# Sandwich block with attention-like scan and top-2 experts, one core: first statistics of batches 4 to 7 and the second tile table placed ahead of tile 0

## The reference

```python
# x: 8 batches x 512 tokens x 128
x = x + layernorm(attn(layernorm(x)))
x = x + layernorm(ffn(layernorm(x)))

def attn(x):                      # a scan over the tokens, not softmax attention
    inp = mix * x + (1 - mix) * shifted(x)          # shifted by one token
    h = relu(inp @ W_in.T + b_in)
    state_t = state_{t-1} * decay + h_t             # along the 512 tokens
    return states @ W_out.T + b_out

def ffn(x):                       # 8 experts, 128 -> 512 -> 128, top 2
    weights = softmax(top2(x @ gate))
    y_e = (silu(x @ w0[e]) * (x @ w1[e])) @ wo[e]
    return sum over the two chosen experts of weight * y_e
```

## Time and profile before

| | us |
|---|---|
| median of 3 executions | 274.52 (274.36 to 274.54) |
| profiled execution | 274.19 |
| its span, first to last instruction | 272.4 |
| TensorE busy | 243.0 (89%) |
| VectorE busy | 186.1 (68%) |
| ScalarE busy | 179.0 (66%) |
| GpSimd busy | 167.2 (61%) |

### The profile page before, as it was taken

One profiled execution on the slowest core, in us unless ns is written; L12 is line 12 of the kernel. 1 busy time (PEld: TensorE's weight loads), 2 busy tenths in 40 slices (PEclk: granted clock), 3 DMA queues, 4 the chain that ended last, 5 costly groups with the idle time before them and its releaser, 6 DMA issues.

```text
span 272.4 us, 8097 instructions
## 1 busy us (share of the span) xinstructions
PE 243.0 (89%) x2059; PEld 231.2 (85%) x2059; DVE 186.1 (68%) x815; ACT 179.0 (66%) x517; POOL 167.2 (61%) x190
## 2 busy tenths in 40 slices
PE   7948778899898999999999999999999999999800
PEld 2738655799898999999999999999999999999700
DVE  4886876877785785687578687844353434998774
ACT  2185869577576777785867587655656566568581
POOL 3317774773678878778878878776333324277740
PEclk9997799999999999999999999999999999999955
DMA  5999961413301321132123113433322108403048
GB/s 174 300 358 375 292 215 51 101 52 84 106 32 49 88 84 40 62 96 65 40 71 101 49 45 108 110 90 89 82 78 70 51 28 331 178 16 96 13 152 231
DMA packets 29675, 31.70 MB, mean 116 GB/s; under 512 B 4778, under 2 KB 22188, under 8 KB 29504
## 3 DMA queue, kind: packets, MB, share of 16 engines
q1 hardware_dynamic: 24448, 22.56, 27.7%
q0 software_dynamic: 4320, 8.50, 8.9%
q10 hardware_dynamic: 864, 0.13, 0.3%
HBM read 19.58 MB, written 12.05 MB: 116 GB/s over the span
## 4 chain that ended last, share of the span: by engine, by line
PE 73%; DVE 14%; issue 4%; POOL 4%; ACT 2%; DVEq 1%; POOLq 0%
PE bank L1764 40%; PE bank L1801 21%; PE bank L1715 3%; PE bank L1759 2%; DVE sb_early L1001 2%; PE bank L1810 2%; PE bank L1665 1%; POOL expert_rows L524 1%; ACT sb_square L653 1%; DVE sb_w_now L1387 1%; DVEq L1381 1%; DVE sb_rest_stats L983 1%; PE bank L1683 1%; POOL pair_rows L537 1%; DVE sb_x L1016 1%
## 5 line engine op out<-in xcount | busy, mean ns | idle before, releaser
L1764 PE MATMUL bank<-sb_xeT,sb_w_now 128*128 128x128 f32 x1136 | 139.5, 275 | 2.9 <-DVE sb_gated L1368 2.4
L1764 PEld LDWEIGHTS bank<-sb_xeT,sb_w_now 128*128 128x128 f32 x1136 | 133.0, 192 | 3.8 <-issue 3.8
L537 POOL DMA_INDIRECT pair_rows<-sb_y_rows,sb_y_pair x71 | 73.4, 1033 | 53.3 <-ACT sb_y_rows L777 32.3
L1368 DVE TENSOR_TENSOR sb_gated<-bank,sb_silu 128x512 f32<-128x512 f32 x71 | 48.9, 689 | 58.0 <-PE bank L1764 46.8
L524 POOL DMA_INDIRECT expert_rows<-sb_row,sb_place x64 | 64.8, 1012 | 28.9 <-issue 18.1
L1801 PE MATMUL bank<-sb_w_raw,sb_gated 128*128 x568 | 75.7, 276 | 0.4 <-ACT sb_y_rows L777 0.3
L1801 PEld LDWEIGHTS bank<-sb_w_raw,sb_gated 128*128 128x128 f32 x568 | 69.1, 192 | 1.0 <-issue 0.9
L748 ACT ACTIVATE sb_silu<-bank 128x512 f32<-128x512 f32 x71 | 42.3, 595 | 17.2 <-PE bank L1764 16.9
L743 ACT ACTIVATE sb_xeT<-bank 128x128 f32<-128x128 f32 x71 | 19.4, 274 | 40.8 <-PE bank L1759 40.5
L766 ACT ACTIVATE sb_w_now<-sb_w_raw 128x512 f32 x71 | 44.3, 624 | 0.0
L1387 DVE COPY sb_w_now<-sb_w_raw 128x512 f32 x71 | 30.2, 425 | 1.6 <-issue 1.6
(11 more groups left out here) (203 smaller groups left out, 249.8 us busy)
## 6 DMA issues: line engine op xcount, KB each, us to landing
sb_taken_rows<-expert_rows SPq DMA_DIRECT2D x71, 65.5 KB, 1.9
sb_w_raw<-in_L_ffn_w SPq DMA_DIRECT2D x2, 2048.0 KB, 16.2
sb_pairs_early<-pair_rows SPq DMA_DIRECT2D x3, 1024.0 KB, 7.2
out_dram<-sb_x SPq DMA_DIRECT2D x3, 512.0 KB, 3.8
pair_rows<-sb_y_rows,sb_y_pair POOLq DMA_INDIRECT x71, 2.4
sb_x<-in_L_attn_x SPq DMA_DIRECT2D x4, 256.0 KB, 4.0
sb_pairs_early<-in_x_turned SPq DMA_DIRECT2D x4, 256.0 KB, 4.2
sb_pairs_early<-in_x_turned SPq DMA_DIRECT2D x1, 1024.0 KB, 7.9
```

The costliest lines, as they stand in the source:

```text
L537: pool.indirect_dma_start(pair_rows[:, :], bass.IndirectOffsetOnAxis(ap=y_pair[group % 2][:, t % PAIRS:t % PAIRS + 1], axis=0), y_rows[slo ...
L1368: dve.tensor_tensor(gated[t % 2][:], p_l2[:], silu[t % 2][:], ALU.mult).then_inc(c["gated"], 1)
L1764: last = pe.matmul(to[:, n * P:(n + 1) * P], w[:, n * P:(n + 1) * P], x, start=True, stop=True)
```

## The change

The order in the front changes, and work of the slots moves into it.

- SyncE loads x of batches 4 to 7 ahead of the two weight loads w0 and w1.
- VectorE: `start1(1)` moves behind `scan(0)`, with the scan waiting for the decays by semaphore; `start1(4)` moves ahead of `offset3(1)`; all of `rest_sums` and `rest_mean_var`, and the reciprocal of batch 4, stand ahead of `residual(2)`; `table_start(1)`, `table_end(1)` and `use_tiles(1)` stand ahead of slot 0; `table_start(2)` moves from slot 2 to slot 1.
- `rest_power` on GpSimd goes; in its place ScalarE takes a root (`rest_root`) and VectorE a reciprocal (`rest_inverse`).
- ScalarE: the means, `root1(4)`, `keep_z(7)` and the fetch of w0 of tile 0 come earlier, `relu(3)` moves behind the load of the Silu table, and half of `normalise3(2)` stands ahead of slot 0.
- TensorE: fills of 6, 5 and 4 matmuls stand among the products of batches 0 to 2, and `times_folded(7)` comes ahead of `mix_and_turn(3)`.

```diff
             load_turned(4, 4, B)
+            load_x(4, 4, B)
             load_w(0, w0_in)
             load_w(1, w1_in)
-            load_x(4, 4, B)
...
                 send_y(t - 4)
-                if t == STEP:
-                    rest_power()
...
+            def rest_root():
+                act.wait_ge(rest["mv"], 1)
+                act.activation(rest_sd[:], rest_mv[:, :, 1], ACT.Sqrt,
+                               bias=eps[:]).then_inc(rest["sd"], 1)
...
             keep_z(3)
+            mean_of_x(2)
+            mean_of_x(3)
             relu(2)
             root1(3)
             squares(1, 0, G)
@@
             keep_z(4)
             keep_z(5)
-            mean_of_x(2)
+            root1(4)
+            mean_of_x(4)
             squares2(2)
             root2(2)
             keep_z(6)
-            relu(3)
+            keep_z(7)
+            chunk_of(0)
+            fetch_w0(0)
+            rest_root()
             squares(2, 0, G)
             root3(2)
-            keep_z(7)
-            root1(4)
-            mean_of_x(3)
-            mean_of_x(4)
             act.activation(unused[:], eps[:], ACT.Silu)
-            chunk_of(0)
-            fetch_w0(0)
+            relu(3)
+            normalise3(2, 0, G // 2)
 
             for k, s, t in slots():
                 first_part(t)
                 if t == 0:
-                    normalise3(2, 0, G)
+                    normalise3(2, G // 2, G)
...
-                                  ALU.mult)
+                                  ALU.mult).then_inc(s_band, 1)
...
+            def rest_inverse():
+                dve.wait_ge(rest["sd"], 1)
+                dve.reciprocal(rest_rs[:], rest_sd[:]).then_inc(rest["rs"], 1)
...
             def scan(b):
+                if b == 0:
+                    dve.wait_ge(s_band, 3)
...
             decays()
-            start1(1)
             folded_weights()
             scan(0)
+            start1(1)
             scale_z(1)
@@
             choose(1)
+            start1(4)
             offset3(1)
@@
             use_tiles(0)
+            rest_sums(0, (B - REST) * G)
+            rest_mean_var()
+            inverse(1, 4, REST, sd1, rs1)
             residual(2)
             top(2)
             choice(2)
             choose(2)
+            rest_inverse()
             offset3(2)
             put(2)
             tags(2)
-            start1(4)
-            inverse(1, 4, REST, sd1, rs1)
             chunk_of(0)
             fetch_w1(0)
+            table_start(1)
+            table_end(1)
+            use_tiles(1)
 
             for k, s, t in slots():
-                if t == 0:
-                    table_start(1)
-                elif t == 1:
-                    table_end(1)
-                elif t == 2:
-                    use_tiles(1)
+                if t == 1:
                     table_start(2)
@@
-                if t in (STEP - 3, STEP - 2, STEP - 1):
-                    rest_sums((t - STEP + 3) * G, (t - STEP + 4) * G)
-                elif t == STEP:
-                    rest_mean_var()
...
             times_folded(2)
+            fill(bank[4], 6)
             ranks(0)
+            pe.wait_ge(a["hidden"], 2)
+            fill(bank[5], 5)
             times_w_out(1)
             times_folded(3)
             mix_and_turn(2)
             times_folded(4)
             ranks(1)
             times_folded(5)
+            pe.wait_ge(a["hidden"], 3)
+            fill(bank[5], 4)
             times_w_out(2)
             times_folded(6)
+            times_folded(7)
             mix_and_turn(3)
-            times_folded(7)
             ranks(2)
```

More of the change, by code:

```diff
@@ L483, in late_power @@
                                    ALU.pow).then_inc(a[f"late_rs{k}"], 1)
-            def rest_power():
-                pool.wait_ge(rest["mv"], 1)
-                pool.tensor_tensor(rest_sd[:], rest_mv[:, :, 1],
-                                   eps[:].broadcast_to([P, (B - REST) * G]),
-                                   ALU.add).then_inc(rest["sd"], 1)
-                pool.wait_ge(rest["sd"], 1)
-                pool.tensor_tensor(rest_rs[:], rest_sd[:],
-                                   minus_half[:].broadcast_to([P, (B - REST) * G]),
-                                   ALU.pow).then_inc(rest["rs"], 1)
             def split_bias():
```

## The result

| us | before | after |
|---|---|---|
| median of 6 executions | 274.53 (274.19 to 274.86) | 272.16 (271.30 to 273.52) |
| profiled execution | 274.19 | 271.30 |
| its span | 272.4 | 269.5 |
| start of tile 2 / tile 14 | 47.23 / 88.29 | 49.00 / 85.25 |
| tile 2 to tile 14 | 41.06 | 36.25 |

The ratio of the times is 0.9919, with an interval of 0.9892 to 0.9946: the kernel became 2.4 us faster (0.8%). The forecast was 272.3 us. The single executions of the kernel after lie 2.2 us apart, those of the kernel before 0.7 us here; over more executions the kernel before spreads as much (2.4 us over the 25 timed beside the last experiments). The profiled execution of the kernel after is the quickest one of the six, so what its trace shows need not be what the median had.

What follows compares the result with a forecast made beforehand. TensorE, always busy from 88 to 250 us, was taken as the bound, so tile 14's start decides: +2.9 at tile 2, -5.16 in the loop, -2.3, giving a median of 272.3 us; range of this case 271.5 to 273.3.

Steps and rivals of the forecast that it cites:

- TensorE bounds everything from tile 14 on: TensorE is busy 162.00 of 162.00 us from 88 to 250 us, so only tile 14's start counts.
- 5.16 us of stalls go: Between tiles 2 and 14: 1.94 us lost from 2 to 8 and 3.22 from 8 to 14, all counted as gone.
- (d): VectorE after tags(2): start1(4), its wait and reciprocal, 1.9 us, are gone; w1 of tile 0 comes +1.5, at 44.2.
- GpSimd stays in front of the residual: GpSimd's queue before batch 4's power: 4.4 us freed, the later loop start takes some 2.9, so it stays ahead.
- (a): VectorE's first scan goes before start1(1), exposing waits of 0.7 and 0.4 us: +0.8 for residual(0), bounds -0.5 and +1.1.
- (b): VectorE: start1(4), 1.4 us, moves ahead of offset3(1) in place of a 0.81 us wait: offset3(1) and scan(2) +1.3.
- the clock holds: Rival, 0.12: the new fills keep the full clock in round 1, about 1.0 us gained ahead of residual(1): 271.3 us.
- (c): VectorE: all rest statistics stand ahead of residual(2) in place of a 0.67 us wait; residual(2) +4.0, between +3.9 and +4.3.
- (e): VectorE: eight more short table 1 instructions, 1.4 us, ahead of scan(3): scan(3) comes +2.9, tile 2 at 50.1.
- Cold fills: Rival, 0.25: the ten fills before tile 0 take 4.5 us at 1.2 GHz, tile 2 at 51.6: 273.7 us.
- The sum: Tile 14: +2.9 at tile 2, -5.16 in the loop, -2.3; 271.9 for the profiled execution, 272.3 us as a median.

Runs made afterwards that it cites:

- stats_back: The changed kernel with the statistics of batches 5 to 7 back in slots 5 to 8 and their power back on GpSimd: 271.92 us, ratio 0.9923.
- table_back: The changed kernel with table 1 back in slots 0 to 2 and table 2 back in slot 2: 272.27 us, ratio 0.9932.
- both_back: The changed kernel with the statistics, their power and table 1 all back in the slots: 273.31 us, ratio 0.9932 to the kernel before.
- before_fills: The kernel before with only the three new fills (6, 5 and 4 matmuls) and the waits for relu ahead of two of them: 273.43 us, ratio 0.9933.
- power_back: The changed kernel with only the power back on GpSimd in slot 8, the statistics still in front: 273.40 us, ratio 0.9977.
- no_new_fills: The changed kernel without the fills of 6, 5 and 4 matmuls: 272.92 us, ratio 0.9936 to the kernel before.
- warm_bridge: The changed kernel with 22 fills ahead of ranks(2) in place of ten behind it: 271.24 us, ratio 0.9885.
- best: The kernel of all_three with nine fills behind tile 0's transpose in place of two, and table 2 in slots 3 to 5: 269.68 us, ratio 0.9812.
- all_three: The changed kernel with 22 fills ahead of ranks(2), scan(3) ahead of table 1, and start1(1) back before the first scan: 270.26 us, ratio 0.9842.

## Why the prediction was right, point by point

- **TensorE bounds everything from tile 14 on.** Right (161.71 of 161.75 us busy).
- **5.16 us of stalls go.** Right in the sum, within 0.35: 4.81 went. The 3.22 from tile 8 on is shown by stats_back, which brings 3.27 back. That I gave the whole 1.94 of the part from 2 to 8 to the table's move was wrong: table_back and both_back bring only 0.4 to 0.5 back. Once table 1 lies further ahead of tile 2, by step (d) or, as in before_fills, by the clock, most of the wait is gone with the table where it was.
- **GpSimd stays in front of the residual.** Not quite: residual(4) waited 0.94 us; VectorE's slack hid it. power_back shows that the slack ends there.
- **(a) +0.8 for residual(0).** 16.16 against 15.32: +0.84. Counted from the decays it is +1.03, since this execution had begun a little earlier.
- **(b) +1.3 for offset3(1).** Measured +0.26 (29.14 against 28.88). The step itself was right: start1(4) stands there in place of the wait. What came on top is the clock in round 1, which gave residual(1) back 1.0 us (24.73, where (a) alone would have put it at 25.7). That was the rival "the clock holds". Its 271.3 us is a median; for the profiled execution it makes 270.9, and 271.30 was measured.
- **(c) +2.7 from there to residual(2).** 37.79 - 34.85 = 2.94, less 0.26: 2.7.
- **(d), (e).** w1 of tile 0 came at +0.34 (+1.5 was forecast) and scan(3) at +1.8 (+2.9 forecast): both 1.1 to 1.2 early, of which 1.0 is the clock's, else as worked out. Tile 2 came at 49.00 behind it, +1.8.
- **Cold fills.** The idle time ahead of ranks(2) was 5.36 us and the ten fills took 3.85, between the 2.33 of the forecast and the 4.5 of the rival, and tile 1 started at 45.77. They cost this execution nothing at tile 2: times_w_out(3) started at 47.97, right behind scan(3) (46.71 + 1.20). By the clock gate rule of the Trainium skill ("TensorE: Matmul & The Clock Gate", Part 1: activity releases the throttle) the fills start cold; the trace agrees, with a clock of 0.50 at 43 us and 1.00 again before they end here, and with all ten at half clock in no_new_fills (4.43 us).
- **The sum.** In the profiled execution tile 2 came 1.1 us earlier than forecast, by the clock, the loop gave 0.35 less, and behind tile 14 it took 0.15 more: 271.30 against the 271.9 of the forecast for it. The median is 272.16, at the 272.3 of the forecast, though the clock held in the one execution that has a trace. That the median meets the forecast to 0.1 us is therefore partly luck: something of about the same size went the other way in the other executions. A clock that fell in round 1 (as in warm_bridge) or fills that were all cold (as in no_new_fills) could do it; neither was seen in a trace of this kernel.

What the prediction had not seen is what the parts are worth one by one. The moves of table 1 and of the statistics of batches 5 to 7 with their power are worth about 0.4 us of the 2.4 by the ratio, which the noise can't tell from nothing or from 1.4. The order in (a) is a loss of about 2 within it, where 0.8 was forecast. The fills, which the forecast counted at nothing, are worth 0.5 to 0.8 in the changed kernel, inside the noise, and 1.5 to 1.8 alone in the kernel before, clear of it.

## What to carry to other kernels

When work is moved from a stage into the stretch in front of it, count both: here 3.27 us of stalls paid for a start 2.5 us later, and only because one 2.3 us instruction left a busy queue on the way. Read a wait as a distance between two engines: it can shrink through an edit that never touches its cause, and undoing the edits one by one and in pairs, and putting single ones into the kernel before, is what shows whose gain it was. Where TensorE has gaps of some microseconds in a chain, look at the granted clock behind each gap; closing one gap moved the loss to the next one. Even in best the clock was at 0.50 from 27.7 to 31.1 us, under the statistics, where it cost nothing on VectorE's path. And a profile is one execution: count from a common point in the chain, and don't let a difference between two traces stand for one of the medians.

## What the runs showed of the hardware

- The same instructions got another clock from execution to execution. The change, warm_bridge and table_back have the same instructions on TensorE through round 1; in their profiles the first drop to 0.50 behind 13 us began at 13.9, 19.9 and 19.6 us, and the products of batch 1 took 1.19, 1.73 and 1.64 us. In no_new_fills the clock was at 0.50 from 20.1 to 26.9 us.
- After an idle stretch of 5.36 us ten fills of 512 columns took 3.85 us; without one, 22 took 4.91. Behind a gap of 1.46 us after two fills the products of all_three ran at half clock (3.26 us for 16), while behind one of 1.91 us at the same place in warm_bridge they ran at full clock (1.95 us): the length of the last gap alone didn't decide.
- GpSimd's power over 12 columns took 2.30 us (2.51 in power_back) and over 4 columns 1.04 to 1.28, while ScalarE's root (0.30) and VectorE's reciprocal (0.22) of the same 12 took 0.5 together.
